# A two-layer graph attention kernel: new order of the first products, the weight transposes and the pair products, and single-value gathers in groups of six

## The reference

```python
def layer0(x, adj, pairs, Wq, bq, Wk, bk):          # 8 heads of 64
    sub, obj = pairs[:, 0], pairs[:, 1]
    q = (x[sub] @ Wq.T + bq).reshape(-1, 8, 64)
    k = (x[obj] @ Wk.T + bk).reshape(-1, 8, 64)
    att = ((q * k).sum(-1) / sqrt(64)).T
    scores = zeros(8, n, n); scores[:, sub, obj] = att
    scores = where(adj == 0, -inf, scores); scores[:, i, i] = 1e-7
    return softmax(scores, 2).sum(0) / 8 @ x
x = layernorm(x + layer0(x, ...))
x = layernorm(x + layer1(x, adj, W_seq, a1, a2, W_out, b_out))   # 16 heads, additive scores, elu
```

## Time and profile before

| | us |
|---|---|
| three runs: lowest, median, highest | 415.62, 417.47, 419.23 |
| the profiled execution | 415.19 |
| its span on the core | 413.4 |
| busy in the span: PE, DVE, ACT, POOL | 350.9, 320.1, 201.5, 187.5 |
| mean clock granted to PE, as a share of full speed | 0.957 |
| last gather of `adj` issued | 125.90 |
| first residual sum (L1767) starts | 169.28 |

### The profile page before, as it was taken

One profiled execution on the slowest core, in us unless ns is written; L12 is line 12 of the kernel. 1 busy time (PEld: TensorE's weight loads), 2 busy tenths in 40 slices (PEclk: granted clock), 3 DMA queues, 4 the chain that ended last, 5 costly groups with the idle time before them and its releaser, 6 DMA issues.

```text
span 413.4 us, 5205 instructions
## 1 busy us (share of the span) xinstructions
PE 350.9 (85%) x1652; PEld 214.9 (52%) x1652; DVE 320.1 (77%) x810; ACT 201.5 (49%) x451; POOL 187.5 (45%) x178
## 2 busy tenths in 40 slices
PE   1799899999992999699999991669979999999970
PEld 1445545545441444288878780446644665566540
DVE  2989999966804874687787857699899999999762
ACT  3975764566230112446555332111346676767780
POOL 7655857776572200000000005787878877880000
PEclk9999999999997799999999996689999999999995
DMA  7999444537990130481112114765666666763113
GB/s 259 380 381 362 153 156 120 188 103 165 266 207 25 52 103 0 159 322 58 55 52 78 54 53 146 210 182 171 166 179 177 186 189 196 212 197 103 43 53 136
DMA packets 34757, 65.10 MB, mean 157 GB/s; under 512 B 15648, under 2 KB 16800, under 8 KB 32672
## 3 DMA queue, kind: packets, MB, share of 16 engines
q1 hardware_dynamic: 25632, 42.45, 30.8%
q0 software_dynamic: 9088, 22.20, 19.4%
HBM read 53.50 MB, written 8.52 MB: 150 GB/s over the span
## 4 chain that ended last, share of the span: by engine, by line
DVE 32%; PE 24%; POOL 16%; DMA 13%; issue 8%; ACT 4%; SPq 0%; DVEq 0%; ACTq 0%; POOLq 0%
PE ps L827 13%; POOL pr L528 8%; POOL adjT L605 8%; DVE adjT L1969 8%; DMA pr<-in_adj_dram,aidx 7%; PE ps L635 5%; DMA arenaA<-in_x_dram 3%; DVE arenaC L1836 2%; DVE adjT L1834 2%; DVE ps L1894 2%; DVE ps L1887 2%; DVE arenaA L1900 2%; PE ps L678 2%; PE ps L816 2%; DVE stage L1959 2%
## 5 line engine op out<-in xcount | busy, mean ns | idle before, releaser
L635 PE MATMUL ps<-arenaB,adjT 128*128 128x512 f16 x512 | 117.9, 389 | 1.8 <-DVE arenaB L1305 1.8
L528 POOL DMA_INDIRECT pr<-in_adj_dram,aidx x79 | 82.4, 1043 | 39.8 <-issue 18.2
L605 POOL DMA_INDIRECT adjT<-seqtab,eidx x64 | 76.8, 1201 | 19.5 <-issue 19.5
L941 PE MATMUL ps<-adjT,stage 128*128 128x264 f32 x256 | 67.3, 410 | 18.9 <-DVE adjT L1969 13.0
L635 PEld LDWEIGHTS ps<-arenaB,adjT 128*128 128x128 f16 x512 | 50.5, 100 | 62.9 <-issue 8.5
L605 POOL DMA_INDIRECT adjT<-seqtab,near x16 | 21.4, 1336 | 117.7 <-DMA seqtab<-arenaA 113.0
L941 PEld LDWEIGHTS ps<-adjT,stage 128*128 128x128 f32 x256 | 49.4, 199 | 40.6 <-DVE ps L1894 21.1
L827 PE MATMUL ps<-stage 128*128 128x272 f32 x256 | 61.5, 394 | 0.2 <-ACT stage L1091 0.2
L854 PE MATMUL ps<-adjT 128*128 128x512 f32 x120 | 54.1, 593 | 1.0 <-ACT ps L1122 1.0
L827 PEld LDWEIGHTS ps<-stage 128*128 128x128 f32 x256 | 47.4, 190 | 9.6 <-ACT stage L1091 0.8
L1969 DVE TENSOR_TENSOR adjT<-adjT 128x1024 f32<-128x1024 f32 (+2 forms) x35 | 47.9, 1373 | 1.9 <-ACT adjT L1218 1.9
(11 more groups left out here) (276 smaller groups left out, 486.8 us busy)
## 6 DMA issues: line engine op xcount, KB each, us to landing
stage<-in_adj_dram SPq DMA_DIRECT2D x16, 1024.0 KB, 5.1
seqtab<-arenaA SPq DMA_DIRECT2D x16, 264.0 KB, 2.0
arenaA<-in_x_dram SPq DMA_DIRECT2D x4, 1024.0 KB, 13.3
out_dram<-arenaC SPq DMA_DIRECT2D x16, 256.0 KB, 3.8
arenaB<-in_x_dram SPq DMA_DIRECT2D x1, 1536.0 KB, 10.6
pr<-in_adj_dram,aidx POOLq DMA_INDIRECT x79
arenaC<-in_L_gnn_Wq_dram SPq DMA_DIRECT2D x1, 1024.0 KB, 16.4
arenaC<-in_L_gnn_Wk_dram SPq DMA_DIRECT2D x1, 1024.0 KB, 19.6
```

What stands on the lines that cost most here:

```text
L528: g.indirect_dma_start(out=avals[:, t:t + 1], out_offset=None, in_=adj_flat, in_offset=bass.IndirectOffsetOnAxis(ap=aidx[:, t:t + 1], axis ...
L605: g.indirect_dma_start(out=Grow[:, b % GR, k, :], out_offset=None, in_=seqtab, in_offset=bass.IndirectOffsetOnAxis(ap=source, axis=0)).the ...
L635: ins = t.matmul(bank(4 + b % 2), adjT[:, b, j, :], xsplit[:, w, j, :], start=(j == 0 and w == 0), stop=(j == NB - 1 and w == 1))
L941: ins = t.matmul(bank(2 * (b % 2) + c, HALF), ehot[:, b % 2, k - 1, :], Grow[:, b % GR, k, c * HALF:(c + 1) * HALF], start=False, stop=(k ...
```

## The change

What it does, engine by engine. **SP** issues the last quarter of x ahead of row block 2. **ACT** copies out only the second half of transposed block 0, casts row block 2 behind all of x, and no longer copies q. **DVE** copies out the first half of block 0 behind its first key product, does the other four maxima of listing 0 behind `low(3)` and its short rest behind `low(7)`, and adds both biases to q and k itself. **POOL** has two semaphores in place of four: gathers go in groups of six, the head of a group waits until all of the group two back have landed and, from the fourth group on, for one of PE's blocks; group g waits for block g - 2. Up to twelve are in flight. **PE** turns row block 2 between the last quarters of blocks 0 and 1, turns the weights in four pairs between the first products of block 3, does eight products between `pair_offsets` and `pair_list`, lays no biases, and has its pair products at other places of blocks 14 and 15.

```diff
-    FLIGHT = 4
-    CALM = 16
-    PACE = 6
+    GROUP = 6
...
             load_x(2)
+            load_x(3)
             load_row(2)
-            load_x(3)
             load_row(3)
...
             for t in range(T):
-                if t >= FLIGHT:
-                    pool.wait_ge(c_av[t % FLIGHT], 16 * (t // FLIGHT))
-                if t >= CALM and (t - CALM) % PACE == 0:
-                    pool.wait_ge(ax_made, 2 + (t - CALM) // PACE)
+                group = t // GROUP
+                if t % GROUP == 0 and group >= 2:
+                    pool.wait_ge(c_av[group % 2], 16 * GROUP * (group // 2))
+                if t % GROUP == 0 and group >= 3:
+                    pool.wait_ge(ax_made, group - 1)
                 g.indirect_dma_start(out=avals[:, t:t + 1], out_offset=None, in_=adj_flat,
                                      in_offset=bass.IndirectOffsetOnAxis(ap=aidx[:, t:t + 1], axis=0)
-                                     ).then_inc(c_av[t % FLIGHT], 16)
+                                     ).then_inc(c_av[group % 2], 16)
...
+                if lo == 0 and b == 0:
+                    pe.wait_ge(half_evac, 1)
...
-            def pair_biases():
-                pe.wait_ge(c_b, 32)
-                for w in range(2):
-                    t.matmul(bank(2 * w), ones[0:1, :], pair_bias[w][0:1, :], start=True, stop=False)
...
                 for b in range(2):
                     multiply(b, q * Q, (q + 1) * Q)
-                if q == 2:
-                    turn_rows(2)
+                    if q == 3 and b == 0:
+                        turn_rows(2)
             for b in range(2, NB - 2):
-                multiply(b, 0, Q)
-                multiply(b, Q, 2 * Q)
+                if b == 3:
+                    for k in range(4):
+                        turn_weights(2 * k, 2 * k + 2)
+                        multiply(b, 2 * k, 2 * k + 2)
+                else:
+                    multiply(b, 0, 2 * Q)
                 if 2 < b and b + 1 < SENT:
                     turn_rows(b + 1)
                 if b == 13:
                     pair_offsets()
-                    pair_list()
                 multiply(b, 2 * Q, 3 * Q)
                 if b == 2:
                     turn_rows(3)
+                if b == 13:
+                    pair_list()
                 multiply(b, 3 * Q, NB)
-                if b == 2:
-                    turn_weights()
             multiply(NB - 2, 0, Q)
             pair_places()
             pair_turn()
-            pair_biases()
+            multiply(NB - 2, Q, Q + 2)
             pair_qk()
-            multiply(NB - 2, Q, NB)
+            multiply(NB - 2, Q + 2, 12)
+            pair_rows()
+            multiply(NB - 2, 12, NB)
             count_rows()
             multiply(NB - 1, 0, 2)
-            pair_rows()
-            multiply(NB - 1, 2, 8)
             pair_sums()
-            multiply(NB - 1, 8, 11)
+            multiply(NB - 1, 2, 6)
             pair_scatter()
-            multiply(NB - 1, 11, 13)
+            multiply(NB - 1, 6, 11)
...
                 correct(0)
-                multiply(NB - 1, 13, NB)
+                multiply(NB - 1, 11, NB)
...
-            save_turned(0)
+            act.wait_ge(row_turned, 2)
+            s.copy(adjT[:, 0, 8:NB, :], turn_banks(0)[:, 8:NB, :]).then_inc(row_evac, 2)
...
-                if q == 2:
-                    cast_row(2)
+            cast_row(2)
...
-                    act.wait_ge(pair_pe.sem, pair_pe.after(0, "q"))
-                    s.copy(qsb, bank(0)).then_inc(q_saved, 1)
...
+                if b == 0:
+                    dve.wait_ge(row_turned, 1)
+                    v.tensor_copy(adjT[:, 0, 0:8, :], turn_banks(0)[:, 0:8, :]).then_inc(half_evac, 1)
...
-                dve.wait_ge(q_saved, 1)
+                dve.wait_ge(c_b, 32)
+                dve.wait_ge(pair_pe.sem, pair_pe.after(0, "q"))
+                v.tensor_tensor(qsb, bank(0), pair_bias[0], ALU.add)
                 dve.wait_ge(pair_pe.sem, pair_pe.after(0, "k"))
-                link(v.tensor_tensor(prod, bank(2), qsb, ALU.mult))
+                link(v.tensor_tensor(prod, bank(2), pair_bias[1], ALU.add))
+                link(v.tensor_tensor(prod, prod, qsb, ALU.mult))
...
-            list_top(0, key0, top0, junk0)
             for b in range(NB):
                 low(b)
+                if b == 3:
+                    list_rest(0, key0, top0)
+                if b == 7:
+                    list_top(0, top0, junk0)
```

More of the change, by code:

```diff
@@ L210, in two_layer_graph_attention @@
         c_row = [sem("c_row0"), sem("c_row1")]
-        c_av = [sem(f"c_av{k}") for k in range(FLIGHT)]
+        c_av = [sem(f"c_av{k}") for k in range(2)]
         c_we, c_a12 = sem("c_we"), sem("c_a12")
@@ L244, in two_layer_graph_attention @@
         pair_step = Stage(sem("pair_step"), ["tot", "hot8", "cur", "diag2", "diag", "mx8", "akeep", "vsel"])
-        pair_pe = Stage(sem("pair_pe"), ["off", "list", "rows2", "turn", "q", "k", "cnt", "rows", "sums", "scat", "bad"])
+        pair_pe = Stage(sem("pair_pe"), ["off", "list", "rows2", "turn", "q", "k", "rows", "cnt", "sums", "scat", "bad"])
         A_dve = Stage(sem("A_dve"), [f"hot{c}" for c in range(NCH)] + ["shift", "so", "idx", "prod", "red", "att",
@@ L638, in multiply, with turn_weights @@
                     ins.then_inc(ax_made, 1)
-            def turn_weights():
+            def turn_weights(lo, hi):
                 pe.wait_ge(c_w, 32)
-                for g in range(NW):
+                for g in range(lo, hi):
                     if g >= 2:
@@ L677, in pair_qk @@
                     for k in range(KT):
-                        ins = t.matmul(bank(2 * w), xsoT[:, w, k, :], WT[:, w, k, :], start=False, stop=(k == KT - 1))
+                        ins = t.matmul(bank(2 * w), xsoT[:, w, k, :], WT[:, w, k, :], start=(k == 0), stop=(k == KT - 1))
                     ins.then_inc(pair_pe.sem, 1)
@@ L1330, in listing @@
                 list_keys(b)
+                list_rest(b)
                 list_top(b)
@@ L1342, in count_pairs @@
             def count_pairs():
-                for k in range(FLIGHT):
-                    dve.wait_ge(c_av[k], 16 * len(range(k, T, FLIGHT)))
+                for k in range(2):
+                    dve.wait_ge(c_av[k], 16 * sum(t // GROUP % 2 == k for t in range(T)))
                 link(v.tensor_tensor(scan[:, 0, :], prf[:, :, 0], prf[:, :, 1], ALU.not_equal))
```

9 lines of the change are left out of this document (5 added, 4 removed).

## The result

| | before | after |
|---|---|---|
| median of the runs (lowest to highest), us | 418.00 (415.62 to 419.23), four | 401.65 (401.32 to 402.36), four |
| profiled execution, its span | 415.19, 413.4 | 401.32, 399.5 |
| mean granted clock | 0.957 | 0.959 |
| `pair_offsets` starts | 130.61 | 122.01 |
| first residual sum starts (L1767, now L1777) | 169.28 | 157.10 |

The ratio of the times is 0.9638, with an interval of 0.9585 to 0.969: 3.6% faster. Each set of runs was on one chip and has its own runs of the kernel before: experiments 1 to 4 were one set, 5 to 8 the next, 9 and 10 a third, and experiment 11 with the second run of experiment 2 a fourth, on four different chips.

The account below looks back on a forecast made before the run. POOL's 79 gathers were taken to bound up to `pair_offsets`, then PE and DVE's pair arithmetic up to L1767. Earlier offsets (7.7) plus 3.5 behind them give 11.2: 404.0 profiled, 406.3 from the median, stated 405; range 401.5 to 411.

Parts of the forecast that it names:

- The sum: Whole kernel: span 413.4 less 11.2 is 402.2, or 404.0 with 1.8 around; 7.7 by earlier offsets, 3.5 behind them.
- the part that I had called unchanged: Everything behind the first residual sum (L1767), 244 us, taken to move along unaltered since no line of it is edited.
- the case's own range: Time if the main forecast holds: 402 to 408, for a lead of 1.5 to 3 and a copy of 0.6 to 1.4.
- The first blocks: Start up to block 3: earlier `low`s and weights turned in four pairs end block 3 at 51.8 instead of 54.2.
- The lead of PE: PE from block 3 to `pair_offsets`: the 2.3 us gained are kept without waits, so PE arrives at 122.85.
- The gathers: POOL's gathers in groups of six: no stalls by landings, last value at 120.5, so PE's arrival at 122.85 decides.
- The rule against it: DVE and GpSimd's exclusive port lock: eight key products cost POOL 1.2 each, 9.8 in all, cutting the gain to about 6.
- its row of 73.24: The gather at 73.24 keeps its 0.94 beside a 1.22 key product, cited as the trace not agreeing with the port lock.
- Behind the offsets: `pair_offsets` to the first residual sum: reordered pair products, biases added by DVE; 3.5 us gained there.
- The new wait: PE before `pair_turn`: waits about 2.4 us, to 132.4, for x's rows to land.
- rival b: Clock falls at the new waits, qk at half speed, mostly hidden: gain 9 to 10.5; chance 0.1.
- The wait at rows: PE before `pair_rows`: a second new wait of 1.8 us, since DVE's `diag` is ready at 145.7.

Follow-up runs that it names:

- experiment 1: Kernel before with only the gathers changed: groups of six, two semaphores, waiting for the group two back; 411.12 us, ratio 0.9854.
- experiment 2: Changed kernel with the old gathers, four in flight with the waits of before, all else as changed; first run 413.05 us, ratio 0.9897.
- experiment 3: Changed kernel with the pair products, the biases and ACT's copy of q in the order of before; 406.64 us, ratio 0.976.
- experiment 4: Changed kernel with the weights turned in one piece ahead of block 3; 404.18 us, ratio 0.9682.
- experiment 5: Changed kernel with the gather gate one block looser from the fifth group on and the pair work earlier; 424.42 us against 423.92 of the kernel before.
- experiment 6: Changed kernel with twelve more products of block 14 ahead of `pair_turn`; 424.54 us, ratio 0.9985 to the kernel before.
- experiment 7: Changed kernel with only the gather gate one block looser from the fifth group on; 422.61 us, ratio 0.9982 to the kernel before.
- experiment 8: Changed kernel with the start as before (x's last quarter, block 0 copies, listing 0, turn of row block 2); 424.54 us, ratio 0.9955.
- experiment 9: Changed kernel itself, unaltered, run again on another chip beside the kernel before (422.78); 420.22 us, ratio 0.9934.
- experiment 10: Changed kernel with the looser gate and the earlier pair work, a second time on another chip; 422.7 us, ratio 0.9953 to the kernel before.
- experiment 11: Kernel before itself, unaltered, run again for its trace and spread; 416.44 us against 418.49 of the same kernel beside it, ratio 0.9958.
- the second run of experiment 2: Changed kernel with the old gathers, four in flight, run again on a further chip; 414.3 us, ratio 0.9901 to the kernel before.

## Why the prediction was right

The sum said 404.0 for the profiled execution; it was 401.32. It said 11.2 us earlier at the first residual sum; it was 12.18. Of the 2.7 us between the two times, 1.0 arose up to the first residual sum, nearly all of it before the offsets, and 1.7 behind it, in the part that I had called unchanged. The forecast of 405 was 3.4 above the median of 401.65. That median lies only 0.15 inside the stated range (401.5 to 411) and just under the case's own range (402 to 408), and by the medians the gain was 16.35 us and not 11.2: besides the 1.7, the profiled execution of the kernel before lay 2.8 under its median and that of the changed one 0.3. The path and most of its terms were right; that the time fell inside the range was close.

**The first blocks.** DVE's copy of the first half of block 0 took 0.69 (I took 1.0, between 0.6 and 1.4). Its first `low` started at 13.36 (13.4) and the last ended at 25.75 (26.0). Block 3 ended at 51.0 (16 products, 3.45, behind 47.59), not 51.8: PE reached it 0.3 earlier, and a weight pair cost 0.87, not 1.04. This is the term that was mis-sized. I had read the 1.04 from one row, and that is the busy time of a pipelined group, whose share from start to start is 0.87. Three pairs make 0.5 us. Splitting the weights was worth 1.6 (experiment 4). The old start wasn't isolated, as its run met the stops. With experiments 1 and 4 the traces give the 12.18 us in steps: 4.2 for the groups alone, 2.8 for PE's earlier arrival (124.83 to 122.01, of which the split of the weights is 1.6), and 5.1 for the pair order, the slow q and k of experiment 1 included.

**The lead of PE is kept.** Right: no wait of PE between 54 and 122, so the 3.0 us gained in block 3 (50.56 to 47.59) were still 3.0 at the last row transposes (96.47 to 93.49), from which PE does the same 128 products without a stop. The lead was put at 2.3. Experiment 4 shows the same with the sign turned.

**The gathers.** Right in every step: gather 30 at 51.98 (52.7), the last issue over at 117.0 (117.2), landed by about 119.7 (120.5), no wait for a landing at all. PE's arrival decides, not the gathers, though with only 0.5 us to spare: the offsets can start 1.52 behind DVE's first step (132.98 to 134.50 in experiment 9), and here that was at 119.95. Experiment 2 shows what the groups are worth once the rest is in: 6.8 to 8.0 us at the offsets.

*The rule against it* was read too early as broken, in the prediction and its row of 73.24. The rows above show what happens. The gather at 63.00 began while DVE's product (62.17, 2.29 long) ran, and it ended at 65.28, 0.82 behind the product's end. The one at 91.47 began inside the product of 90.68 and ended at 92.72, 0.82 behind its end. The one at 90.22 began 0.46 before that product and kept its 0.94, and the product its 1.22. So it is in the whole trace: all 13 gathers of POOL that began while a DVE product of two 2048-column tensors ran ended 0.80 to 0.82 behind the product's end. In the kernel before it is the same, and the gather at 73.24 kept its 0.94 while its product began at 73.37, behind it. DVE's reduction of 2.27 at 54.73, which has one input, did not hold the gather at 55.72 (0.95). This agrees with the rule that the prediction cites (the Trainium skill, SBUF — State Buffer), as far as the gather that comes second is concerned. What was wrong is its price of 1.2 for each key product: a gather is held only for what is left of the product when it begins. From gather 30 on seven were longer, by 4.2 us in all, not 9.8 (the sum had 3.4).

**Behind the offsets.** Predicted 3.5, measured 3.58 (38.67 to 35.09), and this closeness is in part luck: it hides errors that cancel. *The list* came 2.41 behind the offsets and not 3.0. *The new wait* at the turn: 2.4 predicted, 2.64 measured. I gave the fall of the clock behind it 0.1 (rival b); it came true, at 0.69. It cost PE 1.4 us on the turn and four products. It cost the kernel next to nothing, for the reason the rival named and experiments 6 and 9 confirm: DVE binds from list to rows, which lie 20.25 apart here and 20.00 in both of those, where the turn, q and k ran at the full clock. k was ready at 141.7 (141.4) and DVE at 140.88 (142.2), so the two were nearly even, and the order of the two was the other way round. *The wait at rows*: 1.8 predicted, 0.37 measured, since PE came late by the slow clock; in experiment 9, at the full clock, it was 1.75. The rows came 22.66 behind the offsets (22.95), the correction 32.32 behind them (32.35). The sum's 3.5 against the kernel before isn't the worth of the pair order by itself: with the stop at the offsets gone the old order has tails of 37.3 and 40.2 (experiments 3 and 1), the new one 34.9 to 35.3 in five traces. In these five the tail is the same whether the clock fell at the turn (0.57 to 0.69) or not (1.00).

**What I had not foreseen** is that the gain depends on the chip. The kernel before waits 5.5 us at the offsets and the changed one doesn't: a delay of PE alone, by up to 5.5 us before that point, would cost the first nothing and the second all of it. That could account for 5.5 of the 12.5 us of delay in experiment 9. It was argued, not shown. The kernel before took 4.8 us more on that chip than at first, which suggests the same stops, but its trace on such a chip was never taken. And its gathers wait for PE's blocks as well (`ax_made`), so that a delay of PE before the last of these gates can reach its offsets too; in experiment 9 POOL stood 4.02 for PE at 93.49, and PE itself then stood 0.97 for the gathers at the offsets. The rest of the lost gain, some 8 us, stays open.

## What to carry to other kernels

Find the arrival of the engine that waits as well as the event that it waits for: here gathers that ended 9.8 us earlier were worth 8.6, up to PE's own arrival, and each microsecond of PE's work ahead of it was worth one. Fill a stop only where the engine that stops is the one that binds behind it; elsewhere the idle time moves on and can take the clock with it (experiment 6). Beside long DVE products of two SBUF tensors, look at which instruction began first before pricing a gather. Take a pipelined operation's price from start to start, and time a tuned kernel on more than one chip before its gain is quoted.

## What the runs showed of the hardware that I had not expected

**Short stops can cost clock, and need not.** A stop of 1.91 was followed by a granted clock of 0.59 (experiment 3). The same stop was followed by 24 products at the full rate in experiment 1, where the clock fell to 0.57 only behind a further stop of 0.99. At the turn, stops of 2.64, 2.77, 2.52 and 2.79 were followed by 0.69, 0.58, 0.57 and 0.64 over four microseconds (the changed kernel, experiments 4, 7 and 8), and one of 2.59 by 1.00 (experiment 9), as was one of 2.00 (the second run of experiment 2). Before the rows a stop of 4.15 was followed by 0.50 (experiment 6), and stops of 1.75 and 1.82 by 1.00 (experiment 9, the second run of experiment 2). So a fall behind a short stop varies between executions of one kernel, and no run here shows what decides it. The Trainium skill (TensorE: Matmul & The Clock Gate, on HAM oscillation) gives an abstract rule that warns only of idle gaps of PE longer than these of 1.91 to 2.79. The traces agree with it at 4.15, and show that to keep under it isn't enough.

**A gather's issue is held by a DVE product of two SBUF tensors that began before it**, and ends 0.80 to 0.82 us behind the product (13 of 13 in the changed kernel's trace); one that began first is not held.

**Stops that come with the chip or the set of runs.** On two of the four chips of the experiments engines stood still with their work ready: ACT 3.95 and 7.94 us in experiment 9, and 10.46 in experiment 7, with products of PE issued singly 0.3 to 1.5 us apart in others. All traces from these two chips have them, and none from the others. Each chip had one set of runs, so the chip and the time of its set can't be told apart, and all of these traces are of kernels with twelve gathers in flight. The DMA queues weren't full in them: their share was 0.05 from 80 to 90 us in experiment 7. The traces look as if instructions came late to their engines, but the queues that carry instructions moved the same 17 and 20 packets in experiment 9, in the same 0.3% and 0.1% of the span, as in the changed kernel's first trace. None of the runs tests it, and the cause is open.
